# A graph kernel on one NeuronCore: four places instead of two for the tiles of the edge-weighting phase

## The reference: what is computed

```python
ex = jnp.exp(a - amax[dst])                                  # one value per edge and head
den = jax.ops.segment_sum(ex, dst, num_segments=n)
alpha = ex / (den[dst] + 1e-16)
...
h = jnp.concatenate([hs, hv.reshape(e, H, AV * 3)], axis=-1)   # 16 scalars and 8 vectors of 3 per head
agg = jax.ops.segment_sum(alpha * h, dst, num_segments=n)
```

## Time and profile before

| | |
|---|---|
| median of three runs | 3768.85 us |
| the profiled execution | 3771.15 us |
| its span in the trace | 3769.5 us |
| PE busy | 3470.3 us (92%) |
| DVE busy | 3409.4 us (90%) |
| ACT busy | 3056.4 us (81%) |
| POOL busy | 2526.4 us (67%) |
| mean granted clock of TensorE | 0.975 of full |

### The profile page before, as it was taken

How to read it: one execution, slowest core, us unless ns; L and a number is a source line. 1 busy time by engine, 2 the same in 40 slices (tenths; PEclk the granted TensorE clock), 3 DMA queues, 4 the chain that set the end, 5 groups by cost and what they waited for, 6 DMA issues and landing times. The chain is left out here.

```text
span 3769.5 us, 93890 instructions
## 1 busy us (share of the span) xinstructions
PE 3470.3 (92%) x21340; PEld 2652.6 (70%) x21340; DVE 3409.4 (90%) x10190; ACT 3056.4 (81%) x11217; POOL 2526.4 (67%) x2474
## 2 busy tenths in 40 slices
PE   4899999999999999999999939977999999999997
PEld 3888998889988899888998938875333333333335
DVE  5899999999999999999999978876999999999995
ACT  4789999899998999989999947756777878778774
POOL 1777777777777777777777701113777777777772
PEclk8999999999999999999999979997999999999999
DMA  4333333333333333333333349981333333333333
GB/s 111 92 95 99 95 98 98 95 98 96 98 98 95 98 97 97 98 95 99 97 97 97 96 162 278 274 232 52 96 95 96 94 95 95 97 94 96 94 94 116
DMA packets 311032, 414.62 MB, mean 110 GB/s; under 512 B 112692, under 2 KB 245684, under 8 KB 310708
## 3 DMA queue, kind: packets, MB, share of 16 engines
q0 software_dynamic: 127568, 211.04, 22.8%
q1 hardware_dynamic: 183396, 202.83, 17.0%
HBM read 312.70 MB, written 100.94 MB: 110 GB/s over the span
## 5 line engine op out<-in xcount | busy, mean ns | idle before, releaser
L672 POOL DMA_INDIRECT ACC<-src_tab,idx x784 | 837.3, 1068 | 312.9 <-issue 238.5
L739 POOL DMA_INDIRECT ACC<-hid_tab,idx x784 | 808.9, 1032 | 243.8 <-issue 242.9
L672 POOL DMA_INDIRECT TAB<-dst_tab,idx x784 | 779.6, 994 | 238.9 <-issue 238.9
L1145 ACT ACTIVATE MT<-TR 128x768 f32<-128x768 f32 x784 | 610.5, 861 | 3.6 <-PE TR L818 3.6
L868 PE MATMUL HP<-w_hv,MT 128*128 128x128 f32 x3136 | 520.7, 289 | 0.0
L843 PE MATMUL E<-w_mv,MT 128*128 128x128 f32 x3136 | 478.5, 275 | 0.0
L810 PE MATMUL W<-w_rbf,rbf 128*128 128x224 f32 x1568 | 394.7, 375 | 59.6 <-ACT TAB L1134 24.9
L843 PEld LDWEIGHTS E<-w_mv,MT 128*128 128x128 f32 x3136 | 438.5, 192 | 0.0
L1328 ACT ACTIVATE ACC<-TR,y 128x128 f32<-128x128 f32 (+1 forms) x1568 | 418.8, 551 | 8.5 <-PE TR L1003 8.4
L1328 ACT ACTIVATE TAB<-TR,y 128x128 f32<-128x128 f32 (+1 forms) x1568 | 414.0, 423 | 0.0
L868 PEld LDWEIGHTS HP<-w_hv,MT 128*128 128x128 f32 x3136 | 413.7, 192 | 0.0
(11 more groups left out here) (288 smaller groups left out, 8190.6 us busy)
## 6 DMA issues: line engine op xcount, KB each, us to landing
h_tab<-ACC SPq DMA_DIRECT2D x392, 160.0 KB, 2.1
SC<-h_tab SPq DMA_DIRECT2D x50, 640.0 KB, 4.7
TAB<-h_tab SPq DMA_DIRECT2D x48, 640.0 KB, 4.8
ACC<-in_e64T SPq DMA_DIRECT2D x98, 256.0 KB
ACC<-src_tab,idx POOLq DMA_INDIRECT x784
TAB<-dst_tab,idx POOLq DMA_INDIRECT x784
ACC<-hid_tab,idx POOLq DMA_INDIRECT x784, 3.6
agg_tab<-ACC POOLq DMA_DIRECT2D x49, 240.0 KB
```

The lines of the kernel that those rows point to most:

```text
L672: pool.indirect_dma_start(tile[:, v.slot8, g, :], None, table.ap(), bass.IndirectOffsetOnAxis(ap=idx[:, v.sslot, c:c + 1], axis=0))\
L739: pool.indirect_dma_start(gat1[:, v.slot8, g, :], None, hid_tab.ap(), bass.IndirectOffsetOnAxis(ap=idx[:, v.sslot, c:c + 1], axis=0))\
L1145: nc.scalar.activation(dst[:, 0:3].rearrange("p k g e -> p (k g e)"), tr[:, 0:3 * G, :].rearrange("p a e -> p (a e)"), ACT.Copy).then_inc( ...
```

## The change

`HX`, `ohC` and `ex3` get four places each, chosen by the step number modulo 4 (`v.slot`), as `exC` and `hC` have them already. The new places are stretches of ACC that other phases use; `ex3` loses its own tile and moves into ACC too. All waits for `sc` in front of these writes now ask for `sc >= n - 3`, which means that step n - 4 is through. And ACT calls `take_sums(t - 2)` in place of `take_sums(t - 1)`, so that the copy of a sup's sums stands behind the one-hot tiles of three steps later, not two.

```diff
-        HX = flat[:, 0:2 * 8 * HF].rearrange("p (b f) -> p b f", b=2)
-        ohC = flat[:, 2624:2624 + 2 * 8 * P].rearrange("p (b i f) -> p b i f", b=2, i=8)
+        HX = [flat[:, lo:lo + 8 * HF] for lo in (0, 8 * HF, 5248, 5248 + 8 * HF)]
+        ohC = [flat[:, lo:lo + 8 * P].rearrange("p (i f) -> p i f", i=8) for lo in (2624, 2624 + 8 * P, 8400, 8400 + 8 * P)]
...
-        ex3 = sb("ex3", [P, 2, 8 * 3 * H])
+        ex3 = flat[:, 10448:10448 + 4 * 8 * 3 * H].rearrange("p (b f) -> p b f", b=4)
...
-                    ins = nc.tensor.matmul(AGC[v.sslot][:, 0:HF], ohC[:, v.par, i, :], HX[:, v.par, HF * i:HF * (i + 1)],
+                    ins = nc.tensor.matmul(AGC[v.sslot][:, 0:HF], ohC[v.slot][:, i, :], HX[v.slot][:, HF * i:HF * (i + 1)],
...
-                if v.past(2):
-                    act.wait_ge(LC["sc"], v.num - 1)
-                nc.scalar.activation(ax(HX[:, v.par, D:D + 1], (HF, 8), (1, H)), ax(exC[:, v.slot, 0:1], (H, 8), (1, H)), ACT.Copy)
-                nc.scalar.activation(ax(ex3[:, v.par, 0:1], (3 * H, 8), (H, 3), (1, H)),
+                if v.past(4):
+                    act.wait_ge(LC["sc"], v.num - 3)
+                nc.scalar.activation(ax(HX[v.slot][:, D:D + 1], (HF, 8), (1, H)), ax(exC[:, v.slot, 0:1], (H, 8), (1, H)), ACT.Copy)
+                nc.scalar.activation(ax(ex3[:, v.slot, 0:1], (3 * H, 8), (H, 3), (1, H)),
...
-                if v.past(2):
-                    act.wait_ge(LC["sc"], v.num - 1)
+                if v.past(4):
+                    act.wait_ge(LC["sc"], v.num - 3)
                     act.sem_inc(s_passed, 1)
...
-                take_sums(t + -1, total)
-            both(act, lambda sups, wide: loop_steps(act, 2, sups, wide, 1, 1, stage_c))
+                take_sums(t + -2, total)
+            both(act, lambda sups, wide: loop_steps(act, 2, sups, wide, 1, 2, stage_c))
...
-                if v.past(2):
-                    dve.wait_ge(LC["sc"], v.num - 1)
+                if v.past(4):
+                    dve.wait_ge(LC["sc"], v.num - 3)
                 n = 2 * Q - NA
-                TT(ohC[:, v.par, 0:n], ax(iota[:, 0:1], (0, n), (1, P)), places_of(v, 2 * Q * v.place, n),
+                TT(ohC[v.slot][:, 0:n], ax(iota[:, 0:1], (0, n), (1, P)), places_of(v, 2 * Q * v.place, n),
```

More of the change, by code:

```diff
@@ L1246, in one_hots_a @@
                 act.sem_inc(s_passed, 1)
-                nc.scalar.activation(ohC[:, v.par, 2 * Q - NA:2 * Q], far, ACT.Relu, bias=onec[:, 0:1], scale=-1.0)\
+                nc.scalar.activation(ohC[v.slot][:, 2 * Q - NA:2 * Q], far, ACT.Relu, bias=onec[:, 0:1], scale=-1.0)\
                     .then_inc(LC["oha"], 1)
@@ L1778, in weigh_c @@
                 dve.wait_ge(LC["ld"][v.slot], v.slot_round(32, 4))
-                if v.past(2):
-                    dve.wait_ge(LC["sc"], v.num - 1)
-                TT(ax(HX[:, v.par, 0:1], (HF, 8), (16, H), (1, 16)), ax(hC[v.slot][:, 0:1], (D, 8), (16, H), (1, 16)),
+                if v.past(4):
+                    dve.wait_ge(LC["sc"], v.num - 3)
+                TT(ax(HX[v.slot][:, 0:1], (HF, 8), (16, H), (1, 16)), ax(hC[v.slot][:, 0:1], (D, 8), (16, H), (1, 16)),
                    ax(exC[:, v.slot, 0:1], (H, 8), (1, H), (0, 16)), ALU.mult)
                 dve.wait_ge(LC["one"], v.num + 1)
-                TT(ax(HX[:, v.par, S:S + 1], (HF, 8), (8, 3 * H), (1, 8)), ax(hC[v.slot][:, S:S + 1], (D, 8), (8, 3 * H), (1, 8)),
-                   ax(ex3[:, v.par, 0:1], (3 * H, 8), (1, 3 * H), (0, 8)), ALU.mult).then_inc(LC["hx"], 1)
+                TT(ax(HX[v.slot][:, S:S + 1], (HF, 8), (8, 3 * H), (1, 8)), ax(hC[v.slot][:, S:S + 1], (D, 8), (8, 3 * H), (1, 8)),
+                   ax(ex3[:, v.slot, 0:1], (3 * H, 8), (1, 3 * H), (0, 8)), ALU.mult).then_inc(LC["hx"], 1)
             def stage_c(t, total):
```

## The result

The changed kernel takes 3734.23 us, the median of five runs (3730.51 to 3738.46). The kernel before took 3767.49 us beside it (3766.99 to 3769.95, five runs). The ratio is 0.9911, with a 95% interval of 0.9897 to 0.9925: 33 us faster. The profiled execution took 3733.41 us (span 3731.8), against 3771.15 before: 37.7 us less.

A forecast was written before the change was run, and what follows sets the result against it. A ring of PE and DVE waiting for each other bounds the phase at 2.60 us a step. Profiled 3771.15 less 30.3 is 3740.9, the median 2.3 lower, plus about 1 us: forecast 3740, range 3735 to 3753.

The forecast's parts named there:

- The ring between DVE and PE: Phase's main part: PE and DVE wait for each other, 2.60 us a step; four places open it, -30 us.
- PE's pitch of 2.28 us: PE's time for a step that waits for nothing, setting the pitch after the change: 30.3 us less over 95 steps.
- The bounds of the pitch: PE's free step between 2.23 and 2.35 us, giving 35.0 and 23.7 us less; forecast 3734 to 3747.
- The first two steps at 7.35 us: Phase's first two steps, mostly at half clock, 7.35 us for both, left as they are.
- The 1 us added for DVE's uneven pace: About 1 us added to the sum for steps in which DVE's slightly uneven pace is felt.
- The late copy at 0 us: ACT's copy of the sums one step later: 0 us by itself, but without it four places of little use on ACT.
- Register operations at 0 us: Two more on DVE's queue per loop turn of four steps: taken as 0, at most 3 us.
- Transfers: DMA per step: loads 1.70 us plus additions 0.42 us, together 2.12 us, below the 2.28 us pitch.
- 1: Rival: the DMA engines become the wall, pitch falls only to 2.50 us, 9.5 us gained, 3759; chance 0.14.
- 3: Rival: PE's "issue" gaps come from its own queue, not places, so they stay; 3768 or so; chance 0.04.
- 2: Rival: DVE and ACT get into their own ring, pitch 2.41 us, gain 18 us, 3751; chance 0.08.
- 4: Rival: additions landing late hold ACT's copy into `agC`; with 10 us, 42 us slower, 3811; chance 0.04.

The follow-up runs named there:

- third-load kernel: The changed kernel plus a third load in each step, half of the same messages again (320 KB) into free SBUF, awaited by the weighting: 3779.78 us, ratio 1.0024.

## Why the prediction was wrong, and where it was right

- **The mechanism, right.** The ring between DVE and PE opened, PE became the limit, with DVE 0.02 us a step behind it, and PE's idle time went from 20.7 to 0.0 us. The forecast took 30.3 us off the profiled execution and 37.7 came off: 5.0 us more by PE's pitch, 1.15 by the first two steps, 0.39 by the phase's start, 0.73 behind the phase, and 0.1 by the last step.
- **PE's pitch of 2.28 us: the step that failed, by size.** It is 2.227 us, and 95 x 0.053 = 5.0 us more were gained than this term said. I had taken the mean of five rows for pairs of steps (4.74 us) and subtracted one row for a lone step (2.46 us). The shortest of the five rows, 4.69 us, would have given 2.23; the mean's 0.05 us above it is the whole error. What makes the longer rows longer is, in part at least, small waits of PE that the timeline joins without showing them: in the kernel before, the row of 5.08 us at 2292.31 us has no bracket inside, and PE is busy for 4.96 us of it. For the rows of 4.77 and 4.81 us that is inferred, not shown. The 4.69 us are still 0.07 above the 4.62 us of a pair in the changed kernel. That 0.07 us stands in the lone step as well (2.46 us against 4.62 - 2.23 = 2.39) and drops out of the difference. It looks as if the first step after a wait were that much longer. I have not tested this by itself; the third-load kernel, where PE stalls again, has lone steps of 2.46 to 2.49 us too.

```profile
2361.39 2.47 PE L916 MATMUL W<-ACC 128*128 128x164 f32 x16 [0.56 <-DVE ACC L1787]
2364.07 2.49 PE L916 MATMUL HP<-ACC 128*128 128x164 f32 x16 [0.20 <-issue]
```

- **The bounds of the pitch, right, and the range drawn against them.** The lower bound was 2.23 us. Its time of 3734 leaves out the 1 us that the sum adds (3771.15 - 35.0 - 2.3 + 1 = 3734.9), and the upper bound's comes to 3746, not 3747. The range began at 3735, so at the bound itself or above it, and left nothing for the spread of the runs.
- **The first two steps at 7.35 us, taken as fixed.** They took 6.00 to 7.31 us in the traces of this study with all eight matmuls and no identity matmuls. In the changed kernel's first trace the granted clock was 0.50 until 2267 us and 1.00 from 2268 us on, a mean of 0.73 against 0.63 before. That it came out 1.15 us shorter is luck, since the same kernel took 6.99 us in its second trace.
- **The 1 us added for DVE's uneven pace, wrong.** DVE had no part in it; with 0.3 us of waiting for ACT in the whole phase there was nothing to add.
- **The late copy at 0 us, right,** and its reason, that it was needed, wrong. At 0.5 us of the phase it could have stayed where it was.
- **Two of the three tiles' new places at no cost, right, and at a gain of 0.8 us at most.** The prediction did not ask which tile was needed. It was the one-hot tiles.
- **Register operations at 0 us, right.** DVE's step takes 2.21 us as before.
- **Transfers, right that they are no wall at this pitch.** The 2.12 us was too high (about 1.85, by the third-load kernel). By an estimate from the Trainium skill, page "DMA: Bandwidth & Descriptors", section "Bandwidth", whose rows are for DMAs issued by GpSimd, a load of 640 KB would move at 138 to 341 GB/s. That was no bound for several loads in flight: the changed kernel moved 308 GB/s and the third-load kernel 386.
- **Of the rivals,** 1 and 3 fell with the pitch of 2.227 us, 2 and 4 with 0.3 and 0.6 us of waits. The third-load kernel adds that the loads limit the step only at 2.69 us and 1041 thousand bytes.

The median's gain of 33.3 us lies between the forecast's 28.9 and the 37.7 us of the two profiled executions; the later session of the same kernel gave 39.1 us (3730.18 against 3769.25). Why one kernel's medians differ by 4 us stays open. The phase is not where it lies: its main part is the same in both traces of the changed kernel (213.93 us), while the part behind the phase took 1247.83 and 1246.23 us.

## What to carry to other kernels

Before doubling all buffers of a ring, ask which wait stands first in the waiting engine's own order: in this kernel only that tile's places counted, and one place more than two was all it needed. Read an engine's free pitch from the shortest repetition that shows no wait, not from a mean over rows that may hide one. And let the range reach past the bound of the term that decides.

## What the runs showed of the hardware that was not expected

- A DMA share of 0.96 to 1.07 stood beside 264, 308 and 386 GB/s in one and the same phase. The share is time in which packets are under way; here it did not tell how much more could be moved.
- TensorE's clock fell to 1.2 GHz after an idle gap of 2.47 us that came behind 9.8 us of matmuls, and not at once but when matmuls were running again. After a gap of 1.43 us behind 11.3 us of matmuls it stayed at 2.4 GHz. That is one trace each, and the gap and the matmuls ahead of it changed together, so which of the two kept the clock up is not shown.
